# Expert tiles of a mixture-of-experts kernel: the order of ScalarE's and VectorE's work on three tiles at once

## What is computed

```
scores = sigmoid(x @ router_w)
top_k_index = 8 experts of 32 for each token, out of the 4 best of 8 groups
tkw = 2.5 * scores at top_k_index, divided by their sum
gate = ragged_dot(xs, w_gate, group_sizes)
up = ragged_dot(xs, w_up, group_sizes)
down = ragged_dot(silu(gate) * up, w_down, group_sizes)
routed = (down[unsort].reshape(T, K, H) * tkw[..., None]).sum(axis=1)
shared = silu(x @ sw_gate) * (x @ sw_up) @ sw_down
return x + routed + shared
```

## Time and profile before

| what | value |
|---|---|
| median of 3 runs | 1066.85 us (1064.3 to 1068.14) |
| the profiled execution, its own time | 1066.63 us |
| its span in the profile | 1064.8 us |
| mean granted TensorE clock | 0.934 of full speed |
| TensorE matmul busy | 918.4 us, 86% of the span |
| VectorE, ScalarE, GpSimd busy | 577.8, 487.4, 437.2 us |
| memory traffic | 149.25 MB, mean 140 GB/s |

### The profile page before, as it was taken

The page is one execution under the profiler, slowest core; times in us unless marked ns, Lnnn a source line. Parts: engine busy times, 40 slices in busy tenths (PEclk is TensorE's granted clock), DMA queues, the critical chain, the costliest instruction groups (busy, mean ns, idle before and its releaser), DMA issues.

```text
span 1064.8 us, 21255 instructions
## 1 busy us (share of the span) xinstructions
PE 918.4 (86%) x4604; PEld 495.4 (47%) x4605; DVE 577.8 (54%) x1320; ACT 487.4 (46%) x993; POOL 437.2 (41%) x348
## 2 busy tenths in 40 slices
PE   3258698879787999999999999999999999999994
PEld 1143354545343555554545545555544554545542
DVE  5958898889764443446343454444455454453321
ACT  5276563742132443446444454444455454463331
POOL 2011101110032455555655554645545565655643
PEclk8569888798888999999999999999999999999998
DMA  5211120111338578777887778687887787876654
GB/s 170 75 41 52 40 87 7 40 43 40 102 107 268 117 165 178 164 170 206 186 199 145 176 164 218 125 205 176 179 207 173 220 181 210 184 168 122 122 103 72
DMA packets 90267, 149.25 MB, mean 140 GB/s; under 512 B 9648, under 2 KB 46768, under 8 KB 90224
## 3 DMA queue, kind: packets, MB, share of 16 engines
q0 software_dynamic: 33120, 80.64, 38.6%
q1 hardware_dynamic: 57104, 68.13, 19.5%
HBM read 101.55 MB, written 47.20 MB: 140 GB/s over the span
## 4 chain that ended last, share of the span: by engine, by line
PE 47%; issue 9%; DVE 5%; ACT 4%; DVEq 3%; ACTq 3%; DMA 1%; SPq 0%; POOL 0%; POOLq 0%
PE bank L258 40%; PE bank L1484 4%; PE bank L1475 3%; ACT gu L240 3%; DVEq L1170 2%; ACTq L1170 2%; DVE gu L247 1%; DMA stage_dn<-in_L_ffn_w_down_dram 1%; DVE hid L1400 1%; DVE dn L250 1%; DVE hT L1409 1%; ACT silu L1263 0%; PE bank L1456 0%; ACTq L240 0%; DVE mark_p L400 0%
## 5 line engine op out<-in xcount | busy, mean ns | idle before, releaser
L258 PE MATMUL bank<-gu,xgT 128*128 x1764 | 408.6, 382 | 11.9 <-issue 7.6
L1213 POOL DMA_INDIRECT out_dram<-y,ids_i x145 | 242.2, 1671 | 283.4 <-DMA out_dram<-y,ids_i 156.9
L258 PEld LDWEIGHTS bank<-gu,xgT 128*128 128x128 f16 x1764 | 173.1, 98 | 193.7 <-issue 22.9
L258 PE MATMUL bank<-dn,hT 128*128 x870 | 212.1, 380 | 15.9 <-issue 15.8
L1201 POOL DMA_INDIRECT xg<-xrows,ids_i x153 | 158.8, 1038 | 64.2 <-issue 41.4
L1400 DVE SCALAR_TENSOR_TENSOR hid<-bank,xg,silu 128x256 f32<-128x256 f32 x146 | 70.3, 482 | 207.3 <-ACT silu L1263 207.3
L1275 ACT CAST hT<-bank 128x256 f16<-128x256 f32 x146 | 53.7, 368 | 224.9 <-PE bank L1475 224.9
L1282 ACT ACTIVATE y<-bank 128x512 f32<-128x512 f32 x145 | 86.6, 597 | 133.5 <-PE bank L258 133.5
L1409 DVE TENSOR_TENSOR hT<-bank,hT 128x256 f16<-128x256 f32 x146 | 61.7, 423 | 150.7 <-ACT hT L1275 150.7
L258 PEld LDWEIGHTS bank<-dn,hT 128*128 128x128 f16 x870 | 85.0, 98 | 90.6 <-issue 23.3
L247 DVE SCALAR_TENSOR_TENSOR gu<-stage_gu,gu (+1 forms) x64 | 75.6, 1222 | 48.1 <-ACT gu L240 48.1
(11 more groups left out here) (217 smaller groups left out, 770.2 us busy)
## 6 DMA issues: line engine op xcount, KB each, us to landing
stage_gu<-in_L_ffn_w_gate_dram SPq DMA_DIRECT2D x32, 512.0 KB
stage_gu<-in_L_ffn_w_up_dram SPq DMA_DIRECT2D x32, 512.0 KB
stage_dn<-in_L_ffn_w_down_dram SPq DMA_DIRECT2D x32, 512.0 KB
x_sb<-in_x_dram SPq DMA_DIRECT2D x4, 1024.0 KB, 6.9
xrows<-adj SPq DMA_DIRECT2D x4, 1024.0 KB, 4.2
out_dram<-acc SPq DMA_DIRECT2D x4, 1024.0 KB, 4.7
xg<-xrows,ids_i POOLq DMA_INDIRECT x153, 4.4
out_dram<-y,ids_i POOLq DMA_INDIRECT x145, 5.1
```

What stands on the lines that cost most here:

```text
L258: last = nc.tensor.matmul(out_ap, stationary(a, c), moving(w, c), start=(c == 0 and (a, w) == parts[0]), stop=(c == chunks - 1 and (a, w) ...
L1213: g_.indirect_dma_start(out, bass.IndirectOffsetOnAxis(ap=ids_i[:, t:t + 1], axis=0), y[:, t % YS, :], None, compute_op=ALU.add).then_inc( ...
```

## The change

In the step of ScalarE and of VectorE, gates moves back by one place and forward by one tile. Step t was gates(t), split_rows(t+2), next_weights(t), hidden(t); it is now split_rows(t+2), next_weights(t), gates(t+1), hidden(t), and ScalarE's result(t-1) stays last. gates(0) is written ahead of the first step on both engines. TensorE, GpSimd and SyncE have the code they had.

```
@@ -1283,14 +1283,15 @@
                 split_rows(0, 0)
                 split_rows(1, 1)
+                gates(0, 0)
 
                 def step(t, i):
 
 
                     s = i % 2
-                    gates(t, s)
                     split_rows(t + 2, s)
                     next_weights(t)
+                    gates(t + 1, 1 - s)
                     hidden(t, s)
                     if not (isinstance(t, int) and t < 1):
                         result(t - 1, 1 - s, (i + 1) % YS)
@@ -1411,12 +1412,14 @@
                 dve.wait_ge(S["tables_ready"], 1)
                 split_rows(0, 0)
                 split_rows(1, 1)
+                gates(0, 0, 0)
+
                 def step(t, x):
 
                     s = x % 2
-                    gates(t, s, x)
                     split_rows(t + 2, s)
                     next_weights(t)
+                    gates(t + 1, 1 - s, (x + 1) % XG)
                     hidden(t, s)
```

## The result

| what | before | after |
|---|---|---|
| median of 4 runs, on the same chip | 1067.08 us (1064.3 to 1068.14) | 1053.76 us (1052.7 to 1055.25) |
| the profiled execution, its own time | 1066.63 us | 1052.70 us |
| its span in the profile | 1064.8 us | 1050.9 us |
| mean granted TensorE clock | 0.934 | 0.935 |

The ratio is 0.988, with a 95% interval from 0.9857 to 0.9903: 13.3 us faster. Forecast were 11.0 us and a time of 1055.6, which is 1.8 us too high, well inside the range of 1047 to 1063.

The account below looks back on a forecast made before the run. TensorE, busy 86%, was taken as the bound, with conversions the only sizeable stall in the tiles. 1066.6 - 9.9 (product sooner) - 1.1 (conversion starting earlier) = 1055.6 us; range 1047 to 1063.

Parts of the forecast that it names:

- the 4.96 of the forecast: Expected length in us of the step where the transposes wait for the product after a conversion, in place of 5.29.
- second term: ScalarE's conversion starts 0.16 to 0.17 us earlier where its four-step loop has just turned: 7 x 0.16 = 1.1 us.
- first term: On VectorE after a conversion, the product starts 0.33 us sooner, no longer behind the low inner rows: 30 x 0.33 = 9.9 us.
- What the change does to a plain step: nothing: In steps without a conversion, engines issue the same instructions per tile and the step stays at 4.54 us; no gain counted.
- The clock dip: TensorE's granted clock falls to 0.66 for 5 us after the second step's wait, about 1.7 us lost; left in.
- The reading of the down product's lag: TensorE's sequencer does not pass waiting transposes, so the down product's table load, 0.31 us, and what follows are exposed.
- The whole stall: At conversions, both halves of the stall vanish: 30 x 1.55 = 46.5 us, so 1020.1 us; chance 0.03.
- half of it: Table load and wait for the product's share show on VectorE at conversions: gain 5 us, 1061.6 us; chance 0.07.
- no change: What ends the transposes' wait is something the order leaves alone, so the time stays; chance 0.07.
- An earlier conversion everywhere: On ScalarE the conversion starts earlier in all 30 cases: gain 18.3 us, 1048.3 us; chance 0.12.
- The slower case: Low inner rows, pushed behind the product on VectorE, delay the down product by 0.39 us: 11.7 us, 1078.3 us; chance 0.05.
- its bound of 0.73: Reaction time in us from low inner rows' end to down product, under which their later place costs nothing at all.

Follow-up runs that it names:

- Experiment 2: Kernel before the change, with only VectorE in the new order; ScalarE does its silu of t+1 last in the step: 1055.55 us, ratio 0.9893.
- experiments 1 and 3: Two runs of one program, the kernel before with only ScalarE in the new order: 1062.67 us (ratio 0.9956) and, in one run, 1063.9 us.
- experiment 3: Kernel before the change with only ScalarE in the new order, profiled a second time: 1063.9 us in one run, against 1067.13.
- experiment 5: Kernel before the change, with only TensorE's table read for the down product moved ahead of the transposes of the inner rows: 1041.17 us, ratio 0.9758.
- experiment 4: Changed kernel, plus TensorE's table read for the down product moved ahead of the transposes of the inner rows: 1035.16 us, ratio to before 0.9694.
- experiment 9: Changed kernel plus two unused table reads in each VectorE step, making its loop 293 instructions: 1144.21 us, ratio 1.0727.

## Why the prediction was right, and where it was short

**The mechanism held in each of its steps.** The product starts 0.08 to 0.09 us before the end of the last low part in all 30 conversions, where it started 0.25 or 0.26 after it: 0.33 sooner, as counted. The low inner rows follow it. The transposes and the down product keep their distances (0.06 and 1.07 in the example), so the transposes' wait fell to 5.5 us ("5 or 6") and the "issue" idle stayed at 15.3 ("near 15"). Plain steps take 4.54. At the example the step of the wait takes 4.80: the 4.96 of the forecast less the 0.16 of its second term, since this is a conversion at a turn of ScalarE's loop. Experiment 2 has the effect with VectorE's order alone; with ScalarE's, experiments 1 and 3 have none of it at the conversions.

**The conversions gave 8.9 us, not 11.0: the second term did not come.** The 8.9 are those of 29 conversions; the first one, by experiment 3 against the change, has another 0.3 among the first two steps. The 0.33 of the first term holds in each. The 7 x 0.16 of the second holds in four of the seven conversions that it names, which start 0.12 to 0.15 us earlier, counted from the transposes before them; one is unchanged, and two start 0.22 and 0.27 later, so that the seven give 0.1 us and not 1.1. Over the 29 conversions the cost of the two steps changed by -0.96 to +0.40 us, with -0.35 as the median. In the step of the wait the change is -0.33 and whatever the end of the last low part moved against the transposes before it (within 0.02 us in 26 of 29); these steps give 9.4 us, and the steps behind them take 0.5 back, for a reason that stays open. What moves the last low part is in most cases the two table loads that ScalarE's sequencer does before a conversion. They take 0.27 to 0.31 us in most cases and up to 0.97 in some, and from the second load's end it is 0.62 to 0.73 us to the conversion in all 30, in both kernels. The same conversion before and after, in the rows of these loads (least, median and longest in ns, time of start in us):

```profile
L1170 ACTq TENSOR_LOAD <-tile_info x2: 281/282/283, 861.2 to 861.9; - x2
```

```profile
L1170 ACTq TENSOR_LOAD <-tile_info x2: 283/560/838, 851.4 to 852.7; - x2
```

Here one load took 0.56 us longer and the conversion began 0.56 later. The forecast had no term for it, and why a load is long in one execution and short in another stays open.

**"What the change does to a plain step: nothing" was too short.** It is true of a step inside the loop, and missed the 8 plain steps at TensorE's loop turns (2.1 us) and the 1.3 us in the last steps. I had written that the product comes a whole step early (in a plain step it is 2.0 us) and looked only at who waits for it. Who profits is TensorE's sequencer: with the product ready 3.3 us ahead and not 1.3, it has issued the transposes early and gets through the turn (0.51 us of idle before) and its table load while the engine still works. Experiments 1 and 3 take the turns to 0.0 with ScalarE's order alone, experiment 2 keeps 1.2 of the 2.1, and experiment 5 also has 0.0, with the product where it was but a table read less behind the transposes. So it is the sequencer's lead that counts, and the product was one of the two things that held it back. The 1.3 us of the last steps stay open: neither half has them alone (7.4 us became 7.5 in experiment 3 and 7.2 in experiment 2, 6.1 in the change).

**The clock dip was in the range, not in the sum.** It gave about 1.6 of the 2.0 us in the first two steps. By experiment 3 the same program has it or not, so leaving it out was defensible. That it fell away in the profiled execution of the change is luck as far as the runs tell; it is a part of the 13.3 that another execution may not show.

So the number is close in part by luck: 2.1 us too much and some 5 us not counted are errors that offset each other, and 2.3 us net are left between 13.3 measured and 11.0 forecast.

**The reading of the down product's lag was right.** The prediction said that the sequencer does not pass the waiting transposes and that the table load behind them is exposed, against the Trainium skill (Perfetto Trace Analysis, Tensor Engine Instruction (MATMUL, LD_WEIGHTS)). Experiments 4 and 5 moved that load ahead: 18.6 and 26.0 us. By the Trainium skill's rule the move would have brought nothing, as the load would run under the wait in any case; the measurement decides.

**The rivals.** The whole stall and half of it are out by the size, and half of it also by the product's start; no change is out by the interval. An earlier conversion everywhere is out by the timelines (its 18.3 us took a start distance of 0.28 where the earlier trace rows have 0.27, which changes nothing). The slower case did not come: in the changed kernel the down product starts 0.73 us after the end of the low inner rows (501.74 to 502.47), held by the table load. The reaction that the rival asks for is 0.20 us, read in experiment 4 where no table load stands between, and so far under its bound of 0.73 for "costs nothing"; over the 30 conversions of the changed kernel the distance is 0.53 to 0.88. Only with the table load out of the way does the place of the low inner rows cost something, the 0.2 us of experiment 5.

## What to carry to other kernels

When one engine waits for the late result of another, look at what stands between that result and the long job ahead of it, and put there nothing that has slack; the shift of one start is then the gain of each occurrence. Then look at the waiting engine's own sequencer: reading a table entry or a register ahead of the wait and not behind it was worth twice as much as the reordering here. And count a loop's instructions before adding to it.

## What the runs showed that I had not expected

**A loop that outgrows something in the instruction supply.** VectorE's loop with 240 and 245 instructions runs with 30 and 33 instruction packets over the execution; with 293 and 310 it takes 110 and 114 packets and stalls of up to 6.9 us, 90 us in experiment 9. The limit lies between 245 and 293; where was not tried. The Trainium skill (Advanced Engine Details and Errata, ISA Cache) gives the store as two lines of 256 instructions each. The measured limit lies near the length of one line and well under two. That need not contradict the two lines: by these figures a loop a little longer than one line can lie in two or reach into a third, by where it begins, and no run here varied the place of the loop. The Trainium skill (Runtime: NRT & Kernel Launch, Instruction fetch mechanics) says that a taken branch to a target outside the two lines has to fetch it before it goes on. The packets (33 and 110) agree with that; its price in this kernel is the 90 us above.

**The cost of a table read behind a wait.** The load itself is 0.30 us in the sequencer (501.6, above), but taking it and the register work with it out of the way shortened product to down product from 1.05 us, the mean over the 30 conversions, to 0.33 in each (experiment 5), and took the loop turns along. And a load is not always 0.30 us: 0.56 us more of it on ScalarE put a conversion back by as much, and 0.99 us of it on TensorE held a loop turn.

**One program, two clocks at the start.** Experiments 1 and 3 are the same kernel; in 341 to 346 us the granted clock was 0.66 in the one profile and 1.00 in the other, for about 1.6 us.
